# A spiking feed-forward kernel: the order of its loads, its idle row, and 96 places with a turned second layer

## The reference

```python
def cond(inputs, initial_state):              # x [2, 2048, 512], cond [2, 512]
    c = initial_state[:, None, :] + cumsum(relu(inputs) * 0.001, axis=1)
    fl = floor(c)
    prev = concatenate([floor(initial_state)[:, None, :], fl[:, :-1, :]], axis=1)
    return (fl - prev) / 0.001                # a spike where the sum passes a whole number

def ffn(s, w1, b1, w2, b2):                   # w1 [512, 2048], w2 [2048, 512]
    return relu(s @ w1 + b1) @ w2 + b2

out = x + ffn(cond(x, cond_1024), w1, b1, w2, b2)
```

## Time and profile before

| what | value |
|---|---|
| median of 3 runs | 103.96 us (103.45 to 103.97) |
| span of the profiled execution | 102.1 us |
| PE busy | 95.4 us (93%) |
| PEld busy | 54.0 us (53%) |
| DVE busy | 65.9 us (64%) |
| ACT busy | 35.5 us (35%) |
| POOL busy | 43.2 us (42%) |
| HBM read, written | 21.58 MB, 10.75 MB |
| DMA rate while loads run | 376 to 420 GB/s per slice |

### The profile page before, as it was taken

How to read it: one execution, slowest core, us unless ns; L and a number is a source line. 1 busy time by engine, 2 the same in 40 slices (tenths; PEclk the granted TensorE clock), 3 DMA queues, 4 the chain that set the end, 5 groups by cost and what they waited for, 6 DMA issues and landing times.

```text
span 102.1 us, 1157 instructions
## 1 busy us (share of the span) xinstructions
PE 95.4 (93%) x370; PEld 54.0 (53%) x370; DVE 65.9 (64%) x142; ACT 35.5 (35%) x64; POOL 43.2 (42%) x44
## 2 busy tenths in 40 slices
PE   5999999999999999999969999999999999999910
PEld 5944444444644444644234564649999984444300
DVE  2448999888699999488958888899993020020020
ACT  2796515315372540569740000003953330000000
POOL 6350000000078700017508181499937883688040
PEclk9999999999999999999999999999999999999996
DMA  1999999999999999999999725427999999998701
GB/s 58 286 387 414 417 420 411 411 407 409 409 409 409 396 393 401 409 394 387 379 373 352 324 116 218 193 125 292 395 430 436 407 336 195 218 115 106 92 8 62
DMA packets 10028, 31.66 MB, mean 310 GB/s; under 512 B 1671, under 2 KB 1799, under 8 KB 8994
## 3 DMA queue, kind: packets, MB, share of 16 engines
q1 hardware_dynamic: 8304, 29.63, 74.7%
q0 software_dynamic: 1568, 1.90, 11.4%
q10 hardware_dynamic: 146, 0.01, 0.1%
HBM read 21.58 MB, written 10.75 MB: 316 GB/s over the span
## 4 chain that ended last, share of the span: by engine, by line
PE 50%; DVE 20%; POOL 13%; issue 11%; ACT 1%; POOLq 1%; DVEq 0%
PE ps_table L807 40%; DVE x_sb L673 11%; POOL out L347 11%; PE ps_small L900 4%; DVE same L600 3%; PE ps_idle L823 2%; PE ps_turn L844 2%; DVE hot L619 1%; PE ps_idle L827 1%; PE ps_idle L833 1%; DVE spk_t L634 1%; POOL out L381 1%; POOL general_x L370 1%; POOLq L258 1%; DVE spk_t L629 1%
## 5 line engine op out<-in xcount | busy, mean ns | idle before, releaser
L807 PE MATMUL ps_table<-w_sb 128*128 128x512 f32 x128 | 56.9, 595 | 0.0
L807 PEld LDWEIGHTS ps_table<-w_sb 128*128 128x128 f32 x128 | 23.6, 190 | 27.1 <-issue 26.4
L342 POOL DMA_INDIRECT rates<-in_x_turned,sixteen_at x8 | 9.9, 1236 | 33.9 <-DVE sixteen_at L563 32.1
L354 POOL TENSOR_TENSOR x_sb<-x_sb,idle_row 128x512 f32<-128x512 f32 x12 | 14.9, 1277 | 9.9 <-DVEq L706 3.7
L422 ACT ACTIVATE w_sb<-w_sb,b_col 128x512 f32<-128x512 f32 (+2 forms) x19 | 12.2, 643 | 16.5 <-DMA w_sb<-in_w_pairs 16.3
L549 DVE SCALAR_TENSOR_TENSOR total_two<-x_sb,total_two 128x1024 f32<-128x1024 f32 x14 | 17.1, 1225 | 1.2 <-DMA x_sb<-in_x 0.8
L347 POOL DMA_INDIRECT out<-w_sb,to_single x8 | 12.5, 1558 | 5.8 <-issue 3.7
L895 PE MATMUL ps_table<-w_sb 128*128 128x512 f32 x32 | 14.0, 595 | 0.0
L423 ACT ACTIVATE w_sb<-w_sb,minus_relu_b 128x512 f32<-128x512 f32 (+2 forms) x19 | 12.3, 649 | 0.6
L673 DVE TENSOR_TENSOR x_sb<-x_sb,ps_idle 128x2048 f32<-128x2048 f32 x5 | 11.2, 2283 | 1.5 <-ACT idle_row L448 1.3
L895 PEld LDWEIGHTS ps_table<-w_sb 128*128 128x128 f32 x32 | 6.0, 190 | 7.2 <-issue 6.9
(11 more groups left out here) (113 smaller groups left out, 65.5 us busy)
## 6 DMA issues: line engine op xcount, KB each, us to landing
x_sb<-in_x SPq DMA_DIRECT2D x16, 512.0 KB, 14.3
out<-x_sb SPq DMA_DIRECT2D x8, 1024.0 KB, 4.1
w_sb<-in_w_pairs SPq DMA_DIRECT2D x15, 512.0 KB, 15.7
w_sb<-in_w SPq DMA_DIRECT2D x4, 1024.0 KB, 15.3
w_sb<-in_w_pairs SPq DMA_DIRECT2D x2, 256.0 KB, 2.9
b_row<-in_b SPq DMA_DIRECT2D x1, 256.0 KB, 15.3
rates<-in_x_turned,sixteen_at POOLq DMA_INDIRECT x8, 6.5
out<-w_sb,to_single POOLq DMA_INDIRECT x8
```

The costliest lines, as they stand in the source:

```text
L342: pool.indirect_dma_start(out=rates[:, col, :], out_offset=None, in_=x_sixteen, in_offset=bass.IndirectOffsetOnAxis(ap=sixteen_at[:, col:c ...
L354: last = pool.tensor_tensor(x_sb[b][:, t, :], x_sb[b][:, t, :], idle_row[:, :], ALU.add)
L807: last = pe.matmul(ps_table[c][:, :], table_hidden[:, m, c * P:(c + 1) * P], w2_sb[:, m, :], start=(m == 0), stop=(m == FC - 1))
```

## The change

Both weights get layouts of their own, so that a group of chunks is one transfer (groups of one to three). All of w2 is loaded in front of the first piece of x. The idle row is summed by DVE alone, 16 steps accumulating in PSUM, before DVE touches x; one product sums over the partitions, after chunk 3 of the table. The sums over x accumulate in PSUM too. The levels (`rise_levels`) and two lists of names move from DVE to POOL, in more and simpler steps. The idle adds leave DVE's chain to the spikes: POOL does 16 tokens' worth, the first eight while x is still landing, and DVE four pieces after the spikes. The general tokens have 96 places. The second layer is turned: w2's blocks are the weights, the hidden values stream past them, and ACT copies and PE transposes bring the result back.

```diff
@@ SP: loads and stores
+            load_w1_turned(0)
+            load_w2(0)
+            load_w1_turned(1)
+            load_w2(1)
             sp.dma_start(start_c[:, :], cond_cols).then_inc(start_in, 16)
...
+            load_w2(2)
+            load_w1_turned(2)
+            for g in range(3, 7):
+                load_w2(g)
+            for g, begin, end in ((3, 0, 2), (4, 2, 7), (5, 7, 12)):
+                for h in range(begin, end):
+                    load_x(h)
+                load_w1_turned(g)
+            for h in range(12, 16):
+                load_x(h)
+            load_w1_turned(6)
+            load_w1_turned(7)
...
-            for b, q in ((0, 0), (0, 3), (0, 1), (0, 2), (1, 3), (1, 0), (1, 1), (1, 2)):
+            store_idle(0, 0)
+            store_idle(0, 1)
+            for i in range(WQ):
+                load_w1(i)
+            for b, q in ((0, 3), (0, 2), (1, 1), (1, 2), (1, 3), (1, 0)):
                 store_idle(b, q)
@@ POOL
             pool.wait_ge(idle_copied, 1)
...
+            add_idle(0, 0, 8)
+            get_sixteens(0)
+            get_sixteens(1)
+            pool.wait_ge(adding, 1)
+            add_idle(0, 8, 10)
+            pool.wait_ge(adding, 2)
+            add_idle(0, 10, 12)
+            add_idle(1, 0, 4)
@@ ACT
                 table_chunk(m, slice(0, D))
-                if m == 6:
+                if m == 4:
+                    act.wait_ge(idle_summed, 1)
+                    act.activation(idle_row[:, :], ps_idle[:, :], ACT.Copy).then_inc(idle_copied, 1)
+                if m == 7:
                     copy_sums(0)
...
+            for c in range(DC):
+                act.wait_ge(out_turned_summed, c + 1)
+                act.activation(out_turned[c], ps_out_turned[c][:, 0:SLOTS], ACT.Copy).then_inc(out_turned_ready, 1)
@@ DVE
-                step = dve.scalar_tensor_tensor(out=idle_part[:, :], in0=w2_sb[:, m, :], scalar=relu_b1[:, m:m + 1],
-                                                in1=idle_part[:, :], op0=ALU.mult, op1=ALU.add)
-                if m < BY_HAND - 1:
+                step = dve.scalar_tensor_tensor(out=ps_idle[:, :] if m < FC - 1 else idle_part[:, :],
+                                                in0=w2_sb[:, m, :], scalar=relu_b1[:, m:m + 1],
+                                                in1=ps_idle[:, :] if m > 0 else idle_part[:, :], op0=ALU.mult, op1=ALU.add)
+                if m < FC - 1:
...
+                sums = ps_total[:, :].rearrange("p (t d) -> p t d", t=TH)
...
                     if h == 0:
-                        chain(dve.tensor_scalar(total_two[b][:, :, :], tokens, 0.0, None, ALU.max))
+                        step = dve.tensor_scalar(sums, tokens, 0.0, None, ALU.max)
                     else:
...
+                        step = dve.scalar_tensor_tensor(out=sums if h < XH - 1 else total_two[:, :, :], in0=tokens, scalar=0.0,
+                                                        in1=sums, op0=ALU.max, op1=ALU.add)
...
+            for m in range(FC):
+                idle_by_hand(m)
+            block_totals(0, 0, XH)
+            block_totals(1, 0, 2)
             find_blocks(0)
...
+            block_totals(1, 2, XH)
+            find_blocks(1)
             find_bases(0)
...
             find_tokens(0)
             find_bases(1)
             count_met(0)
             find_leads(0)
-            dve.wait_ge(idle_copied, 1)
-            dve.sem_inc(reading_psum, 1)
-            add_idle(0, 0, 4)
             find_tokens(1)
...
             second_spikes()
-            add_idle(0, 8, 12)
-            add_idle(1, 0, 4)
+            add_idle(0, 12, 16)
+            list_singles()
             add_idle(1, 4, 8)
-            list_singles()
             list_general()
+            add_idle(1, 8, 12)
+            add_idle(1, 12, 16)
@@ PE
+            def sum_idle():
+                pe.wait_ge(idle_part_ready, 1)
+                pe.matmul(ps_idle[:, :], ones[:, :], idle_part[:, :], start=True, stop=True).then_inc(idle_summed, 1)
...
-                        last = pe.matmul(ps_hidden[m % 2][:, 0:P], w1_sb[:, c, m * P:(m + 1) * P],
-                                         spk_t[:, c, :], start=(c == 0), stop=(c == DC - 1))
+                        last = pe.matmul(ps_hidden[m % 2][:, 0:n], w1_sb[:, c, m * P:(m + 1) * P],
+                                         spk_t[:, c, 0:n], start=(c == 0), stop=(c == DC - 1))
...
+            def turn_out(c):
+
+                pe.wait_ge(out_turned_ready, c + 1)
+                to = ps_out_last[0:SLOTS, 0:P] if c == DC - 1 else ps_out[0:SLOTS, c * P:(c + 1) * P]
+                pe.transpose(to, out_turned[c], ident[:, :]).then_inc(out_summed, 1)
+
+            def general_layer():
+
+                for c in range(DC):
+                    for m in range(FC):
+                        if c == 0:
+                            pe.wait_ge(hidden_ready, m + 1)
+                        last = pe.matmul(ps_out_turned[c][:, 0:SLOTS], w2_sb[:, m, c * P:(c + 1) * P], hidden[m][:, 0:SLOTS],
+                                         start=(m == 0), stop=(m == FC - 1))
+                    last.then_inc(out_turned_summed, 1)
+                    if c > 0:
+                        turn_out(c - 1)
+                turn_out(DC - 1)
...
+            for m in range(2, 4):
+                table_chunk(m)
+            sum_idle()
+            for m in range(4, 7):
                 table_chunk(m)
             sum_totals(0)
-            for m in range(6, 9):
+            for m in range(7, 10):
                 table_chunk(m)
-            table_chunk(9)
-            table_part(10, 0, 3)
+            table_part(10, 0, 1)
             sum_totals(1)
...
             pe.wait_ge(spk_ready, 1)
             for i in range(WQ):
                 pe.wait_ge(w1_in[i], 16)
-            for last in first_layer(hidden_ready, 0):
+            for last in first_layer(hidden_ready, 0, SLOTS):
                 last.then_inc(hidden_summed, 1)
             sum_checks()
-            second_layer(hidden_ready, 0).then_inc(out_summed, 1)
+            general_layer()
```

More of the change, by code:

```diff
@@ L173, in spike_ffn @@
         ps_checks = ps_table[DC - 1]
+        ps_out_turned = [ps_table[1], ps_table[2], ps_turn, ps_small]
+        ps_out_last = ps_table[1]
         x_in = [[sem(f"x_in{b}_{h}") for h in range(XH)] for b in range(B)]
-        w_in = [sem(f"w_in{m}") for m in range(FC)]
-        w2_first_in = sem("w2_first_in")
+        w1_turned_in = [sem(f"w1_turned_in{g}") for g in range(len(W1_GROUPS))]
+        adding = sem("adding")
+        w2_in = [sem(f"w2_in{g}") for g in range(len(W2_GROUPS))]
         w1_in = [sem(f"w1_in{i}") for i in range(WQ)]
@@ L182, in spike_ffn @@
         const_ready = sem("const_ready")
+        goals_ready = sem("goals_ready")
+        levels_ready = sem("levels_ready")
+        warm_ended = sem("warm_ended")
+        x_summed = [sem(f"x_summed{b}") for b in range(B)]
         ones_ready = sem("ones_ready")
@@ L254, in own @@
             return slice(b * DC, (b + 1) * DC)
+        w1_group = [g for g, (begin, end) in enumerate(W1_GROUPS) for _ in range(begin, end)]
+        w2_group = [g for g, (begin, end) in enumerate(W2_GROUPS) for _ in range(begin, end)]
         def redo_count(eng):
@@ L336, in _, with names, get_sixteens @@
+            def names():
+                pool.wait_ge(const_ready, 3)
+                chain(pool.tensor_copy(slot_name[:, :], slot_i[:, :]))
+                chain(pool.tensor_copy(sixteen_f[:, :], sixteen_i[:, :]))
+            rise_levels()
+            names()
+            pool.sem_inc(levels_ready, 1)
             last_row = pool.to_reg(ROWS - 1)
-            for b in range(B):
+            def get_sixteens(b):
                 pool.wait_ge(sixteen_listed, b + 1)
@@ L618, in find_slots @@
                                                in1=leads[:, mine], op0=ALU.add, op1=ALU.mult))
-                chain(dve.tensor_tensor(hot[:, mine, :], over(slot[:, mine], P), along(slot_name[:, :], DC), ALU.is_equal))
+                chain(dve.tensor_tensor(hot[:, mine, :], over(slot[:, mine], SLOTS), along(slot_name[:, 0:SLOTS], DC), ALU.is_equal))
                 dve.sem_inc(hot_ready, 1)
@@ L628, in first_spikes @@
                 dve.wait_ge(slots_found, 1)
-                chain(dve.tensor_tensor(spk_t[:, :, :], over(token[:, own(0)], P), along(ps_slots[:, 0:P], DC), ALU.is_equal))
+                chain(dve.tensor_tensor(spk_t[:, :, 0:SLOTS], over(token[:, own(0)], SLOTS), along(ps_slots[:, 0:SLOTS], DC), ALU.is_equal))
             def second_spikes():
@@ L726, in _ @@
             dve.wait_ge(b2_in, 16)
-            chain(dve.tensor_tensor(general_x[:, :], general_x[:, :], b2_row[:, :], ALU.add))
-            dve.wait_ge(out_summed, 1)
-            dve.tensor_tensor(new_row, ps_out[:, :], general_x[:, :], ALU.add).then_inc(row_ready, 1)
+            chain(dve.tensor_tensor(general_x[0:SLOTS, :], general_x[0:SLOTS, :], b2_row[0:SLOTS, :], ALU.add))
```

(15 more changed lines are left out.)

252 lines of the change are left out of this document (90 added, 162 removed).

## The result

The changed kernel took 110.33, 112.14, 112.50 and 110.95 us, a median of 111.55, beside 103.97 for the kernel before on the same chip. The ratio, 1.066 with an interval of 1.057 to 1.075, leaves out the slower executions of both kernels: 112.14 and 112.50 here, and one of 207.75 before. Even the shortest time, 110.33, is outside the predicted range of 104.9 to 110.0, on the predicted side. The profiled execution, 110.33 us with a span of 108.6, has no fall of the clock on its path.

What follows compares the result with a forecast made beforehand. TensorE was taken to bound the kernel. Waits less the idle row's saving (+3.0), the turned second layer (+0.9) and its end (+0.3) gave +4.2 on a span of 102.1; with 1.9 beyond the span, 108.1 us, range 104.9 to 110.0.

Steps and rivals of the forecast that it cites:

- The width of narrow products: Both layers: weight loads pace narrow products at 0.1117 us; the rival, that 96 columns run faster, gave 101.6, chance 0.09.
- the idle product: TensorE's product for the idle row, behind 16 table products: it waits 2.4 us for VectorE's sum.
- at chunk 8: Table products of chunk 8: TensorE waits 1.0 us for ScalarE's copy of the sums and two passes.
- at the leads: Count of leads after the spikes: TensorE, done up to chunk 12 by 55.7, waits 1.9 us.
- the price of a first step: VectorE's first step of each batch over x, now writing PSUM: between 0.69 and 1.23 us, taken as 1.23.
- the turned layer with its end: Second layer: 128 loads and three transposes cost +0.9 us, its longer chain to the last add +0.3.
- the second gather: Batch 1's table rows: a rival had them late, up to +0.6 us, 109 to 110 in all, chance 0.10.
- the check of the waits: TensorE up to the first layer: waits of 5.7 and 0.3 for hand-over, less 3.0 for the idle row, give +3.0 us.
- These cost nothing: Idle adds after the spikes, start levels, stores, adding scatters and w1's landing: all in time, no cost.
- chunks 6 to 8 of w2 are now complete with the 14th, so at 13.0: Early weight loads: these chunks land at 13.0, and ten VectorE steps then finish the idle sum at 20.9.
- then 1.23 + 0.69 and TensorE's four products of sums start at 32.4: Batch 0: after x's last piece at 30.3, two VectorE steps release TensorE's sums at 32.4, a wait of 0.2 us.
- its last rival: Batch 1's gathered table rows come late: up to +0.6 us, more if the clock falls; 109 to 110, chance 0.10.

Runs made afterwards that it cites:

- whole groups (and filled waits): Changed kernel with each weight group one whole piece in DRAM and products without use in two TensorE waits; median 110.30 us.
- the three taken away and the waits filled: Changed kernel with weight groups whole in DRAM, GpSimd's first eight idle adds and batch 1's adding scatters left out, unused products in two TensorE waits; median 109.06 us.
- the three terms taken away: Changed kernel with weight groups whole in DRAM, GpSimd's first eight idle adds and batch 1's four adding scatters left out; median 111.48 us.
- filled: Changed kernel with two 512-column products without use ahead of the idle row's product and two ahead of the first count of leads; median 112.51 us.

## Why the prediction was wrong

The direction was right, and the mechanism in the main; the size was not. Between the forecast of 108.1 and the median of 111.55 lie 3.4 us: 2.2 in the execution without a fall of the clock (110.33), and 1.2 in the spread above it.

*Right.* The width of narrow products does not count (128 and 96 columns alike); x comes later and TensorE waits, at the idle product 1.99 (2.4 predicted), at chunk 8 0.58 (1.0), at the leads 1.85 (1.9); the last x lands at 43.5 (43.2); the price of a first step is its upper bound, 1.21; the turned layer with its end is +1.0 to 1.1 by two profiles (1.2); the second gather costs TensorE nothing.

*The step that failed* is the check of the waits, "5.7, with 0.3 for the hand-overs around them; less 3.0 this is +3.0", and behind it "These cost nothing" for the stores and scatters. In the execution without a fall the first layer comes 4.7 us later than before, at 73.60 where the prediction had 71.9, and the span is 108.6, where the sum gave 106.3. Three terms were too small or at nothing:
- "chunks 6 to 8 of w2 are now complete with the 14th, so at 13.0" took the landing from other transfers. They landed at 13.77, the idle product started at 21.79 instead of 21.0, and the last x of batch 0 landed at 31.0 instead of 30.3.
- "then 1.23 + 0.69 and TensorE's four products of sums start at 32.4" took DVE's `total` at its old price. Beside GpSimd's adds, which the change had put there, it is 1.72, and the sums start at 34.14, behind a wait of 0.92 where 0.2 was predicted. From there VectorE has no gap in which to catch up (it takes the last x at 44.46, a microsecond after it landed), and TensorE stays 1.7 behind the forecast, to the first layer's 73.60 against 71.9. With whole groups (and filled waits) the first layer starts at 73.11, without the adds as well at 72.02: these two terms are nearly all of the 1.7.
- "stores and adding scatters end well ahead of 102" is false for the new order: they were issued until 103.05. The last scatter takes 3.5 us instead of 2.7 to land, which is 0.8 of the error, but removing those scatters did not mend it (3.6). Over the kernels with the change it took 3.1 to 5.3; why stays open.

With these, 106.3 + 1.7 + 0.8, less 0.2 by which the turned layer cost less than predicted, is 108.6, the span that was measured. With the three taken away and the waits filled, the profiled span is 106.4.

*The clock.* The check also prices a wait at its own length. The prediction spoke of the clock only under its last rival ("if the clock falls in the waits, some more") and gave it no size. The runs give one: 1.7 us for a fall at the leads, and 0.3 to 0.7 left at the first layer for one at the idle product or the sums. With the three terms taken away, filling the waits moved the median from 111.48 to 109.06. In the changed kernel itself it did not (111.55 and, filled, 112.51). So falls do lengthen executions of such kernels; how much of the 1.2 they are here is not shown. The execution of 112.50 us, at .961, has the mean clock of those with two falls. The one of 112.14, at .979, is as near to the filled one at .980, which had none and a late scatter instead.

## What to carry to other kernels

Price a new wait of some 2 us on a busy TensorE at its length, and beside that give a chance to a fall of the clock behind it: here up to 1.7 us, less where a later wait takes it up, in about half of the profiles at one place. When work moves to an engine that stood idle, look at who runs beside it then: the adds that were moved to GpSimd slowed VectorE's step on the path by 1 us, and VectorE had no gap to make it good. And follow an engine's work to the stores: what comes late there is late at the end.

## What the runs showed of the hardware

- Behind waits of 1.8 to 2.9 us TensorE's granted clock fell to .50, the lower of its two levels, for some 3 to 7 us, in some executions and not in others: at the leads, after the same 1.84 or 1.85 us, in four profiled executions and not in four. At the end, where TensorE is done, it fell in every profile.
- Some of VectorE's steps on SBUF slow down beside GpSimd's adds on SBUF: `total` from 0.69 to 1.72, and back to 0.69 when the adds are left out; and a step on 8 elements a partition from 0.17 to 1.19, which no run tests apart. DVE's timeline after, with POOL adding beside it, and before, just after POOL's adds had ended at 75.07:

```profile
74.67 1.19 DVE L646 TENSOR_SCALAR not_single<-single 128x8 f32<-128x8 f32 x1
...
75.17 0.17 DVE L624 TENSOR_SCALAR not_single<-single 128x8 f32<-128x8 f32 x1
```

- Transfers early in a kernel land by how they lie in DRAM: 512 KB as 128 rows 32 KB apart took 5.3 to 6.4 us from issue in seven profiles, the same in one piece 4.7 to 5.1 in four.
